# A pre-norm attention and SwiGLU layer on one core: the stage ahead of the attention units is laid out anew

## The reference

```python
x = x + layernorm(attn(layernorm(x), q_w, k_w, v_w, o_w, q_b, k_b, v_b, o_b))
x = x + layernorm(ffn(layernorm(x), w_gate_up, w_down))

# attn: q, k, v = h @ w.T + b, 16 heads of 32
scores = einsum('bhqd,bhkd->bhqk', q, k) / sqrt(32)
scores = where(ki > qi, -inf, scores)
out = einsum('bhqk,bhkd->bhqd', softmax(scores), v) @ o_w.T + o_b
# ffn
gate, up = split(h @ w_gate_up.T); out = (silu(gate) * up) @ w_down.T
```

## Time and profile before

| what | value |
|---|---|
| median of 3 runs | 1025.7 us (1022.47 to 1026.97) |
| the profiled execution | 1022.25 us, span 1020.5 us, mean granted clock 0.988 |
| PE busy | 982.3 us, 96% of the span |
| DVE busy | 718.6 us, 70% |
| POOL busy | 683.1 us, 67% |
| ACT busy | 414.2 us, 41% |
| share of the chain that ended last | PE 78%, DVE 9%, POOL 6%, ACT, DMA and issue 2% each |

### The profile page before, as it was taken

One profiled execution on the slowest core, in us unless ns is written; L12 is line 12 of the kernel. 1 busy time (PEld: TensorE's weight loads), 2 busy tenths in 40 slices (PEclk: granted clock), 3 DMA queues, 4 the chain that ended last, 5 costly groups with the idle time before them and its releaser, 6 DMA issues.

```text
span 1020.5 us, 15765 instructions
## 1 busy us (share of the span) xinstructions
PE 982.3 (96%) x5689; PEld 756.7 (74%) x5689; DVE 718.6 (70%) x1421; ACT 414.2 (41%) x720; POOL 683.1 (67%) x492
## 2 busy tenths in 40 slices
PE   5998999999998999989999999999999999999997
PEld 4766767676676676665677888888888888888886
DVE  6675877787587777877778577776665877777722
ACT  3214545555214555555435333332533433333232
POOL 4203888889635999889077966753688668676273
PEclk8998999999999999997999999999999999999999
DMA  6321333332421333321234211112432322211053
GB/s 222 88 83 48 88 95 88 83 88 74 120 93 38 79 90 92 79 70 60 83 104 134 93 63 62 62 62 68 139 114 101 119 69 79 88 62 63 21 155 134
DMA packets 49182, 90.70 MB, mean 89 GB/s; under 512 B 10448, under 2 KB 10960, under 8 KB 48848
## 3 DMA queue, kind: packets, MB, share of 16 engines
q1 hardware_dynamic: 48560, 89.43, 29.0%
q10 hardware_dynamic: 544, 0.26, 0.1%
HBM read 55.84 MB, written 8.39 MB: 63 GB/s over the span
## 4 chain that ended last, share of the span: by engine, by line
PE 78%; DVE 9%; POOL 6%; ACT 2%; DMA 2%; issue 2%; SPq 1%; ACTq 0%; POOLq 0%; DVEq 0%
PE ps L1680 19%; PE ps L1682 19%; PE ps L1681 19%; PE ps L1772 7%; PE ps L1746 6%; PE ps L1806 5%; POOL p_sum L751 2%; PE ps L1820 1%; DMA x_in<-x 1%; PE ps L1780 1%; DMA q_stack<-x_in 1%; DVE xt_lo L1299 1%; DVE stats L1477 1%; DVE p_sum L1285 1%; DVE stats L1482 1%
## 5 line engine op out<-in xcount | busy, mean ns | idle before, releaser
L1322 DVE CUSTOM_DVE_ANT_0 ps<-ps,mask_q 128x384 f32<-128x384 f32 (+7 forms) x256 | 189.9, 779 | 68.2 <-PE ps L1746 65.0
L1772 PE MATMUL ps<-q_stack,k_stack 98*128 98x512 f32 (+3 forms) x384 | 118.7, 387 | 7.2 <-DMA q_stack<-x_in 5.6
L1746 PE MATMUL ps<-k_stack,q_stack 96*128 96x512 f32 (+3 forms) x384 | 109.2, 365 | 1.7 <-DVE m_full L1322 0.9
L773 POOL TENSOR_TENSOR dn_lo<-dn_raw,dn_hi 128x512 fp32r<-128x512 f32 x48 | 66.3, 1381 | 42.9 <-ACT dn_hi L1090 42.9
L1772 PEld LDWEIGHTS ps<-q_stack,k_stack 98*128 98x128 f32 x384 | 63.8, 196 | 31.6 <-DMA q_stack<-x_in 7.2
L1746 PEld LDWEIGHTS ps<-k_stack,q_stack 96*128 96x128 f32 x384 | 67.2, 193 | 27.0 <-DVE m_full L1322 11.4
L818 POOL TENSOR_TENSOR gu_lo<-s_raw,gu_hi 128x1024 fp32r<-128x1024 f32 x27 | 64.9, 2403 | 23.2 <-ACT gu_hi L1162 23.2
L988 ACT ACTIVATE p_own<-ps 128x512 f32<-128x512 f32 x112 | 61.0, 599 | 38.1 <-PE ps L1772 23.5
L988 ACT ACTIVATE x_in<-ps 128x512 f32<-128x512 f32 x112 | 61.2, 598 | 34.7 <-PE ps L1772 22.9
L1185 ACT ACTIVATE silu<-ps 128x512 f32<-128x512 f32 x27 | 16.2, 600 | 141.5 <-DVE ps L1571 141.5
L814 POOL TENSOR_TENSOR a_lo<-gu_raw,a_hi 128x512 fp32r<-128x512 f32 x27 | 35.9, 1331 | 51.7 <-ACT a_hi L1155 51.5
(11 more groups left out here) (226 smaller groups left out, 2821.9 us busy)
## 6 DMA issues: line engine op xcount, KB each, us to landing
gu_raw<-gu_w SPq DMA_DIRECT2D x37, 512.0 KB, 3.6
dn_raw<-dn_w SPq DMA_DIRECT2D x48, 256.0 KB, 2.7
x_in<-x SPq DMA_DIRECT2D x32, 256.0 KB, 4.6
q_stack<-st_hi SPq DMA_DIRECT2D x128, 64.0 KB, 2.0
k_stack<-st_hi SPq DMA_DIRECT2D x128, 64.0 KB, 2.0
qk_raw<-qk_w SPq DMA_DIRECT2D x16, 256.0 KB, 3.0
q_stack<-st_lo SPq DMA_DIRECT2D x64, 64.0 KB, 2.0
k_stack<-st_lo SPq DMA_DIRECT2D x64, 64.0 KB, 2.0
```

The lines of the kernel that those rows point to most:

```text
L773: nc.gpsimd.tensor_tensor(dn_lo[:, s], dn_raw[:, s], dn_hi[:, s].bitcast(F32), ALU.subtract).then_inc(dn_split, 1)
L1322: nc.vector.tensor_tensor_reduce(out=scores, in0=scores, in1=mask_q[:, SEQ - (t + 1) * P:], scale=1.0, scalar=MASKED, op0=ALU.add, op1=ALU ...
L1746: last = nc.tensor.matmul(bank[:, 0:width], q_stack[0:QK_ROWS, s, h, t * P:(t + 1) * P], k_stack[0:QK_ROWS, s, h, half * CH:half * CH + wi ...
L1772: last = nc.tensor.matmul(bank[:, at_col:at_col + n * P], k_stack[0:ROWS, s, h, kt * P:(kt + 1) * P], q_stack[0:ROWS, s, h, t * P:(t + n) ...
```

## The change

The start holds only the eight tiles of the first batch. The tiles of the second batch (called rest) are loaded into a buffer of their own (`rest_raw`, which lies where `xt_hi` of batch 1 will be), summed and squared on ACT with its accumulator (L1121 and L1129 of the new kernel), scaled on ACT in unit 0 (`normalise_rest`, L1003) and transposed by PE in units 1 to 4, two tiles in each (`transpose_rest`, L1789), behind the fourth round of scores. ACT copies them behind the exponentials of the third round, DVE takes the rest of them between the maxima pieces 7 and 8. The first maxima (M) and the last projection (L, by quarters) stand in `START` among the value products, without fillers. P(0, c) waits for the tiles of its half alone. The v and o weights are split by quarters, the o weights late. The v bias is no longer the first load.

```diff
-LAG_X = 2
-AHEAD_X = 6
-PROJECT_AFTER = {TT - 1: ((0, 0),), TT: ((0, 1),), 2 * TT - 3: ((1, 0),)}
...
+LAG_X = 3
+START = [("X", 0), ("X", 1), ("X", 2), ("X", 3), ("V", 0), ("X", 4), ("P", (0, 0)), ("X", 5), ("V", 1), ("X", 6), ("X", 7), ("V", 2),
+         ("P", (0, 1)), ("M", 0), ("M", 1), ("M", 2), ("M", 3), ("V", 3), ("M", 4), ("M", 5), ("M", 6), ("M", 7), ("P", (1, 0)),
+         ("V", 4), ("V", 5), ("M", 8), ("L", 0), ("M", 9), ("V", 6), ("V", 7), ("M", 10), ("L", 1), ("M", 11), ("M", 12), ("L", 2),
+         ("M", 13), ("L", 3), ("M", 14), ("M", 15)]
...
+REST_TILES = {1: (0, 1), 2: (2, 3), 3: (4, 5), 4: (6, 7)}
+REST_AFTER = 8
...
SP:
-            sp.dma_start(v_bias[:, :], v_b.partition_broadcast(P)).then_inc(consts_loaded, DMA)
...
+            for n in range(TT):
                 load_x(n)
-                if n == 1:
+                if n == 2:
+                    load_qk(0)
                     sp.dma_start(vo_raw[:, 0], v_w).then_inc(vo_loaded[0], DMA)
...
+            for t in range(TT // 2):
+                load_rest(t)
+            load_qk(1)
             sp.wait_ge(bank_free, use_of_p(0, 0) + 1)
             load_q(0, 0)
             load_k(0, 0)
-            for n in range(TT + X_SLOTS, 2 * TT):
-                load_x(n)
-            load_qk(2)
+            for t in range(TT // 2, TT):
+                load_rest(t)
             sp.wait_ge(bank_free, use_of_p(0, 1) + 1)
             load_k(0, 1)
             load_q(0, 1)
-            sp.wait_ge(vo_split, 2)
+            load_qk(2)
+            sp.dma_start(vo_raw[:, 1], o_w).then_inc(vo_loaded[1], DMA)
...
POOL:
+            qk_rest(0)
             for n, (hi, lo) in enumerate(((vw_hi, vw_lo), (ow_hi, ow_lo))):
-                pool.wait_ge(vo_hi_done, n + 1)
-                nc.gpsimd.tensor_tensor(lo[:, :, :], vo_raw[:, n], hi[:, :, :].bitcast(F32), ALU.subtract).then_inc(vo_split, 1)
+                for k in range(KT):
+                    pool.wait_ge(vo_hi_done, n * KT + k + 1)
+                    nc.gpsimd.tensor_tensor(lo[:, k, :], vo_raw[:, n, k, :], hi[:, k, :].bitcast(F32), ALU.subtract).then_inc(vo_split, 1)
...
ACT, unit g:
                     exps(g, r)
+                    if r == 2:
+                        for t in REST_TILES.get(g, ()):
+                            hi_of_xt(1, t, use_of_rest(g, t))
...
+                    if g == 0 and r:
+                        normalise_rest(r - 1)
...
ACT, start:
+            for t in range(TT):
+                act.wait_ge(rest_loaded[t], DMA)
+                nc.scalar.activation(rest_tile(t), raw_tile(t), ACT.Copy, accum_out=rest_sum[:, t:t + 1]).then_inc(rest_summed, 1)
+            hi_of_proj(1, 0, use_of_p(1, 0))
             hi_of_qk(2)
+            for k in range(KT):
+                hi_of_vo(1, ow_hi, k)
+            act.wait_ge(rest_summed, TT)
+            act.wait_ge(rest_centre, 1)
+            for t in range(TT):
+                nc.scalar.activation(rest_tile(t), raw_tile(t), ACT.Square, bias=rest_less[:, t:t + 1], accum_out=rest_square[:, t:t + 1]).then_inc(rest_summed, 1)
...
DVE, unit g:
-                    maxima(g + 1, range(EARLY, len(MAXES) - 4))
+                    maxima(g + 1, range(EARLY, REST_AFTER))
+                for t in REST_TILES.get(g, ()):
+                    lo_of_xt(1, t, use_of_rest(g, t))
+                if ahead:
+                    maxima(g + 1, range(REST_AFTER, len(MAXES) - 4))
...
PE:
-                if g == 0 and n > 1:
-                    keep_busy(ST_BANK, 2)
...
                 scores(g, 3)
+                for t in REST_TILES.get(g, ()):
+                    transpose_rest(t, use_of_rest(g, t))
                 project_next(1, 2)
...
-                    pe.wait_ge(bank_free, use_of_xt(TT - 1) + 1)
+                    pe.wait_ge(bank_free, use_of_xt((t[1] + 1) * TT // NCH - 1) + 1)
```

More of the change, by code:

```diff
@@ L55 @@
 BUSY = 2 * P
-BUSY_AT_TILE = {**{_t: 7 for _t in range(1, TT)}, 13: 6, 2 * TT + 15: 3}
+BUSY_AT_TILE = {**{_t: 7 for _t in range(1, TT)}, TT + 15: 3}
 HALF = P * TT // SETS
@@ L98, with banks_of @@
 HI_OF_PARTS = (0, 4, 6)
-LAG_X = 2
-AHEAD_X = 6
-PROJECT_AFTER = {TT - 1: ((0, 0),), TT: ((0, 1),), 2 * TT - 3: ((1, 0),)}
[L105 to L114, removed]
+LAG_X = 3
+START = [("X", 0), ("X", 1), ("X", 2), ("X", 3), ("V", 0), ("X", 4), ("P", (0, 0)), ("X", 5), ("V", 1), ("X", 6), ("X", 7), ("V", 2),
[3 rows of a table added]
+def banks_of(kind, arg):
+    if kind == "M":
+        return MAXES[arg][2]
+    return 0 if kind == "L" else 1 + arg[0] if kind == "P" else 1
+START_AT = {item: sum(banks_of(*before) for before in START[:n]) for n, item in enumerate(START)}
+START_USES = sum(banks_of(*item) for item in START)
+assert all(START_AT[item] % RING + banks_of(*item) <= RING for item in START if item[0] == "M")
+REST_TILES = {1: (0, 1), 2: (2, 3), 3: (4, 5), 4: (6, 7)}
+REST_AFTER = 8
 FIRST_BANKS = MAX_OFF[EARLY]
@@ L163, in use_body @@
 def use_body(g):
[L165 to L168, removed]
+    use = START_USES
+    for before in range(g):
+        use += NCH + (BANKS_MAX if before + 1 < ALL_UNITS else 0) + SUM_BANKS * has_sums(before) + len(REST_TILES.get(before, ()))
+        if before % UNITS == UNITS - 1:
             use += SUM_BANKS + len(MID)
@@ L423, in build @@
         xn_ready = sem("xn_ready")
+        rest_loaded = [sem(f"rest_loaded{t}") for t in range(TT)]
+        rest_summed = sem("rest_summed")
+        rest_centre = sem("rest_centre")
+        rest_scaled = sem("rest_scaled")
+        rest_normed = sem("rest_normed")
         y_ready = sem("y_ready")
@@ L1047, in residual @@
                         slots = range(0 if t < TT else 1, 2 if t else 1)
-                        root((2 + 2 * b) * TT + min(2 * t + 1, 2 * TT), slots[0], len(slots))
+                        root((1 + 2 * b) * TT + min(2 * t + 1, 2 * TT), slots[0], len(slots))
                     extra(t)
-            act.wait_ge(consts_loaded, DMA)
             act.wait_ge(consts_made, 1)
-            for e in range(2 * TT + LAG_X):
-                if e < 2 * TT:
+            done = 0
+            for e in range(TT + 2):
+                if e < TT:
@@ L1512, in _ @@
                     if kind == "X":
[L1513 to L1516 removed]
+                        lo_of_xt(0, t, use_of_xt(t))
+                    elif kind == "V":
+                        if t == 0:
+                            vec.wait_ge(consts_loaded, DMA)
                         values(0, t)
[L1518 removed]
+                    elif kind == "P":
                         lo_of_proj(*t, use_of_p(*t), banks=1 + t[0])
[L1520 to L1521 removed]
+                    elif kind == "M":
+                        if t == 0:
+                            vec.wait_ge(consts_made, 1)
+                        maxima(0, (t,))
+                    if (kind, t) == ("M", len(MAXES) - 2):
+                        lo_of_proj(1, 1)
+                    if n < len(START) and START[n][0] == "X":
+                        break
             for b in range(BATCH):
@@ L1702, in transpose_x, with transpose_rest @@
                 last.then_inc(bank_full, 1)
+            def transpose_rest(t, use):
+                pe.wait_ge(rest_normed, t + 1)
+                bank = ring(use)
+                for k in range(KT):
+                    last = nc.tensor.transpose(bank[:, k * P:(k + 1) * P], x_rest[:, 1, k, t * P:(t + 1) * P], ident[:, :])
+                last.then_inc(bank_full, 1)
             def tokens_by_weights(b, t, hi, lo, use):
```

156 lines of the change are left out of this document (88 added, 68 removed).

## The result

The changed kernel took 1014.54 us (median of 4 runs, 1012.89 to 1017.35) against 1026.03 of the kernel before in the same measurement: ratio 0.9922, 95% interval 0.9895 to 0.9950. Timed again on another occasion it took 1014.88 (6 runs), ratio 0.9932 (0.9908 to 0.9955). So it is faster by 0.7 to 0.8%, some 7 to 8 us by the ratio. The first two medians differ by 11.5, which is too much: in three later measurements the kernel before had medians of 1021.5 to 1022.6. The profiled execution's span is 1013.9 us against 1020.5. The forecast was 1015.7.

The account below looks back on a forecast made before the run. PE bounds the units; the start is bound by PE's waits for DVE, v weights and x. -17.6 + 1.3 + 8.0 = -8.3 us gives 1014.0 (profile) or 1017.4 (median), middle 1015.7; own range 1012 to 1019, overall 1008 to 1022.

Parts of the forecast that it names:

- The front: Start: fewer tiles ahead and v weights by quarters bring the first value product to 16.0 us instead of 24.26.
- the 17.6: Whole start: unit 0 begins at 63.0 us instead of 80.62, a gain of 17.6 us.
- V0's 8.3 us: Start: the part of the gain from the first value product coming at 16.0 instead of 24.26 us.
- the maxima pieces: Start, PE's work before unit 0: 9216 columns, 18 times 512 at 0.23 us, 4.1 us.
- The stacks: Start, SP queue: first maxima's stacks land 11.1 us behind P(0,0), PE has 11.7 us of work; no wait, 0.6 in hand.
- ACT's sums and squares: Start, second batch: sixteen ACT operations, 9 to 18 us, costed at nothing; at 18 unit 0 about 1 us later.
- The term of 1.3: Unit 0: eight scalings of 0.6 us between ACT's exponentials cost 1.3 us, bounds 0 and 4.8.
- Units 1 to 4: Two transposed tiles a unit cost 2.0 us, 0.7 PE's work and 1.3 waits; 8.0 lost in all (2.8 to 16).
- list of signs: First value product near 16, unit 0 starting near 63 and lasting 24.3 to 26, units 1 to 4 about 2 over 25.7.
- (a): Units 1 to 4: the 1.3 us waits are absorbed, 2.8 us lost instead of 8.0; 1010.5 us, chance 0.18.
- (c): Units 0 to 4: POOL's adding becomes the bound, 16 us lost in four units; slower, 1027.2 us, chance 0.07.
- (b): Start gives two thirds: slower clock, late stacks, POOL's quarters; unit 0 at 68, gain 12.6; 1020.7 us, chance 0.15.

Follow-up runs that it names:

- early-load run: Changed kernel with unit 1's q and k weights loaded behind the seventh x load, not behind the eighth and four loads of the second batch; 1014.8 us.
- the one with ten fillers: The version amid the value products with ten fillers ahead of the first value product; 1011.84 us, ratio 0.9892.
- copies later: Changed kernel with ACT's copies of the transposed tiles in units 1 to 4 behind the fourth round's exponentials instead of the third's; 1012.0 us.
- behind piece 11: Changed kernel with the transposes of units 1 to 4 behind maxima piece 11, ACT's copies behind the sixth round's exponentials; 1011.7 us, ratio 0.9886.
- amid the value products: Changed kernel with units 1 to 4's transposes amid the early value products, ACT's copies behind the sixth exponentials, unit 1's q and k load early; 1009.74 us.

## Why the prediction was right, point by point

**The front.** V0 at 16.0 was forecast, 15.71 measured. P(0,0) was to end near 22.5, so to start near 19.6 (the sum's own terms, 2.88 for V0 and 1.15 for X4, give 20.0); measured 20.66, since ACT stood 2.48 us in the copy of unit 1's q and k weights, whose load had been put behind four loads of the second batch. I had not followed that queue. The early-load run shows it as 1.0 us between V0 and P(0,0).

**Where the 17.6 come from.** V0's 8.3 us came (8.55), but from V0 to unit 0 it is 48.99 us after 56.36, a gain of 7.4 where 9.3 was forecast. The 17.6 was 1.7 too large: V0 0.3 early, then 0.9 lost between V0 and P(0,0), the queue's, and 1.1 behind P(0,0), where the sum has 43.0 us (43.2 and 3.8 less V0 and X4) and 44.04 were measured. It was not the waits: the profile lists 3.7 us of them behind P(0,0), 3.8 was forecast for all. The term mis-sized is that of the maxima pieces: added up from PE's timeline they took 6.05 us instead of 4.1, the last pairs 0.63 and 0.73 us where twice 0.23 was assumed; the products took 2.80 instead of 2.88 each. Why the pieces take longer is not shown.

Is the early V0 what the gain stands on? Unit 0 followed P(0,0) by 43.94 to 44.04 us in both profiles of the changed kernel and in the seven variants that keep the order behind P(0,0) without more fillers there: PE has little wait in that stretch and works off a fixed list. With V0 2.4 us later in the same order (v weights in one piece) P(0,0) was 3.3 and unit 0 3.2 later. With V0 4.7 us later and two tiles moved ahead of it, P(0,0) was 2.9 and unit 0 1.4 later. With V0 0.4 later and P(0,0) 6.2 later unit 0 lost 5.6. So V0's lead counts as far as it brings P(0,0) forward, and by itself it is not worth 8.3. To split the gain at P(0,0) instead, 13.96 us ahead of it (34.62 to 20.66) and 2.0 behind it (46.0 to 44.04), is bookkeeping too: the change itself moved V1 and three tiles, some 6 us of PE's work, from ahead of P(0,0) to behind it. Nor does the distance hold for other orders: it was 42.6 us with X5 ahead of P(0,0), and 43.4 with X5 to X7 and V1 ahead and a wait of 5.2 in it. (The prediction's "four of the eight transposes" is a slip: ten tiles stood behind V0 before, four now.)

**The stacks.** Predicted to land 11.1 us behind the end of P(0,0) with 0.6 us in hand. M0 started at 35.38 without a wait, right behind P(0,1) and 14.72 us behind the start of P(0,0). In the two runs in which it did wait, with P(0,0) behind X7 and (by 0.2 us) with V0 later, it came 13.64 and 13.52 us behind that start. So about 1.1 us were in hand; the run with P(0,0) later shows what lies behind them, 5.2 us of wait.

**ACT's sums and squares.** Within the bounds. An activation with its accumulator is two instructions, 0.62 and 0.19 us for a sum, 0.71 and 0.19 for a square, one each 0.61 and 0.71 us:

```profile
36.17 0.62 ACT L1121 ACTIVATE x_rest<-rest_raw 128x512 f32<-128x512 f32 x1
36.69 0.19 ACT L1121 ACTIVATION_READ_ACCUMULATOR x_rest<-rest_raw 128x1 f32 x1
...
62.08 0.69 ACT L985 ACTIVATE st_hi<-ps,qk_bias 128x512 fp32r<-128x512 f32 x1 [2.74 <-PE ps L1762]
```

ACT then waited 2.74 us for PE ahead of the last copy, so they cost nothing here, and they loaded no table of their own.

**Unit 0.** The term of 1.3 was mis-sized: 0.4. The forecast had unit 0 between 24.3 and 26 us; it took 21.60, less than the 23.74 before, since in the profile of the kernel before the clock had fallen in it. This I had not counted on either side, and it is not the change's doing: where the clock falls differs between runs of one order (below).

**Units 1 to 4.** 2.0 us each forecast, 2.1 to 2.3 measured; 8.0 against 8.8. The split was a little off: PE's part is 0.82 to 1.0 us, not 0.70, as a pair of tiles is longer than twice the 0.35 that one had in the start; the waits are 1.2 to 1.4. The mechanism (the bank behind the division, then ACT's copies ahead of the fourth round's exponentials) is in the rows of unit 1, and moving the transposes took 1.0 of it away. The 25.70 us that the prediction calls unit 1 are the window 104.30 to 130.00, which is longer than the unit: by the ruler unit 1 took 22.05 us (106.52 to 128.57), with PE busy for all of it and POOL for 18.56. The reading that PE has no idle time holds; the unit lengths in its list of signs are too long.

**The rivals.** (a), the waits absorbed, is out: nothing gave them back. (c), POOL's chain added on top, is out too: 2.2 a unit, not 4. (b), the start giving less, was partly right in its mechanism, a fall of the clock, but the start itself ran at full clock here, and the fall behind it cost 1.6 us in this profile, 0.8 in the second one (unit 0 at 22.25), 1.0 in the variant without scalings, 2.4 in two, 4.0 in the one with ten fillers, and nothing in five (copies later, behind piece 11, v weights in one piece, amid the value products, P(0,0) behind X7).

**The sum.** -15.9 + 1.6 (clock, in unit 0's head) - 2.1 + 8.8 = -7.6 at unit 5 against -8.3 forecast, and -6.6 at the end of the span. That the sum comes so close is partly luck. The start gave 1.7 less than forecast and units 1 to 4 took 0.8 more; unit 0 with its head made up 1.9 of these 2.5 (-0.6 where +1.3 was forecast), mostly through the fall of the clock in the kernel before, which no term held. The forecast of 1015.7 also lies midway between two starting points, 1014.0 and 1017.4.

## What to carry to other kernels

Look for the event from which the later stage keeps a constant distance, over several variants with the same order behind it; here it was the first projection (44.0 us). An earlier first product helps as far as it brings that event forward. Where a variant moves work across the event the distance changes, and a gain cannot be split there without counting that work. Work moved out of a stage with waits into one where an engine is always busy is paid in full, plus the waits that it meets there; set it amid a long run of that engine's work which needs neither its banks nor its followers, and only the work is left. And when loads are reordered, follow every small one in the same queue: one 256 KB load behind four others held the engine that all copies stood on.

## What the runs showed of the hardware

POOL's subtraction over 2048 columns holds a DVE `tensor_scalar` for its whole length: 4.16 us instead of 0.55 when POOL ran 4.50. The Trainium skill, "SBUF — State Buffer", section "Who interferes with whom", says so, and the trace agrees; beside the quarters the longest was 1.14. One of 1.53 us (from 6.34) ended just behind POOL's memset (4.08 to 7.59); that the memset held it is not shown by an experiment.

The granted clock falls to 1.2 GHz in different places in runs of one order. Between 60 and 90 us it was down at 65 to 70 (0.67) in one profile of the changed kernel, at 70 to 75 (0.67) in the other, and nowhere in the two variants that differ from it only in units 1 to 4. In further variants it was down nowhere, in two windows, or in three (0.66, 0.68, 0.64). Nine matmuls at 0.43 us instead of 0.23 cost 1.6 us, a fall inside unit 0 cost 0.8 to 2.4 (22.25 to 23.88 instead of 21.4). The runs of the changed kernel lie 4.5 us apart; how much of that is the clock's was not measured. More fillers did not lower the median (1011.84 with ten more, 1009.74 without).
